# One kernel for tokenising, attention and a mixture of experts: the first tile of each expert at a fixed place, its loads and the list of tiles reordered, and the centring of the first layer norm moved behind the low half of the mix

## The chip, the cores and the metric

The kernel runs on one core of one Trainium2 chip. The metric is the device time of one execution in microseconds (us); lower is better. The time before is the median of three executions. Five engines work side by side: PE (TensorE, matmuls and transposes), DVE (VectorE), ACT (ScalarE), POOL (GpSimd) and SP (SyncE, which only issues transfers here). Sixteen DMA engines carry out all transfers.

## What is computed

`x` is (128, 750, 32). Everything is float32.

```python
h = patches(x, 16 rows, stride 8) @ W + b           # (128, 92, 128)
n = layernorm(h)                                    # over the last axis
s = einsum('bhie,bhje->bhij', n @ Wk, n @ Wq) / 64  # 8 heads
ax = einsum('bhtf,bhit->bhfi', n @ Wv, softmax(s))
h = h + reshape(ax) @ Wlt                           # (b, f, h*i) read as rows of 1024
t = layernorm(h)                                    # 11776 rows of 128
top2 of softmax(t @ Wr + br), renormalised          # 8 experts
h = h + sum over the two experts of weight * (relu(t @ W1[e] + b1[e]) @ W2[e] + b2[e])
```

## The kernel before

Operands that need float32 accuracy are split in a high half (type fp32r) and a low half, and a product is three matmuls: high by high, high by low, low by high (`three`, L331 to L335). So every intermediate is copied out of PSUM twice, by ACT as the high half and by DVE as the low half.

**First part (about 0 to 850 us), 32 groups of four sequences.** A group has eight steps, one for each sequence and half of the heads; `step(g, k, ...)` of each engine (PE L1387, ACT L801, DVE L1035, POOL L622, SP L448) writes its order out by hand, and different stages of different groups lie in one step. PE makes the scores (L1393), the mix with the probabilities (`mix`, L1405, lines L333 to L335), the transposes of the probabilities (L1418), the values (L1426), and, for the next group, the embedding (L1326), the transposes into token order (L1334) and back (L1340, `turn_xn`, in step 4). DVE in a step: sum of exponentials (L1040), row maximum (L1047), reciprocal (L1054), subtraction of the maximum (L1059), low half of the transposed probabilities (L1068, `probT_l`), low half of the mix (L1075, written into the memory of `w2s`, and so named in the profile). In step 2 it also takes the next group's layer norm moments (L985), its variance plus eps (`keep_var`, L991) and the centring of its tokens (`keep_xcent`, L997, `xcent`), both between L1059 and L1068:

```python
if k == 2 and exists(g + 1):
    keep_var(g + 1)
    keep_xcent(g + 1)
```

PE's mix waits for `probTl_kept` and for the low half of the mix before it (`mixl_kept`). POOL, in step 2, takes the variance to the power -0.5 (L599), multiplies the centred tokens by it (L606, `xtok`; waits for `xcent_kept`) and only then scales the probabilities (L592).

**Second part (about 850 to 1147 us), 23 chunks of 512 rows.** SP loads the chunk's rows and residual (`load_a`, L430, 2048 KB and 256 KB) one chunk ahead. It may issue chunk c+2 when h1 of chunk c is done. PE transposes and projects them, DVE adds the residual (`keep_h1`, L1104), and DVE and ACT do the second layer norm, the router, the top two and the rows' places (`posi`, L1183). `base` holds, for each expert, the row behind its last. Each expert has a room of ROOM = 12288 rows in `sorted_scratch`. POOL scatters the normalised rows of 520 bytes there, eight indirect transfers of 128 rows for each chunk (L709), with one pow between them (`root2`, L702). ACT may write `trow` of chunk c only when the scatters of chunk c-2 have landed (L872).

**The seam (about 1120 to 1156 us).** When the last chunk is counted, DVE copies `base` to `padi` (L1240); SP and ACT each write four pads of 512 blank rows behind the experts' last rows (`lay_pads`, L394 to L400, each with a register load). DVE and PE make the list of the 53 tiles of 512 rows (`whosei`: the expert, `wherei`: the first row; L1241 to L1255, PE L1522 to L1533): expert by expert, all tiles of one before those of the next. SP then (L505 to L521) waits for the list, loads the weights of the first tiles, waits for all pads, for the spare rows and for every scatter, and loads tiles 0 to 2. PE goes on at L1534 after the list, then waits for `posi`, `trow` and `res` of the last chunk.

**Third part (about 1156 to 1500 us), 53 tiles.** For each, SP copies one expert's weights inside SBUF (`w1t` L488, two buffers; `w2t` L495, three; 512 KB each) and loads the rows (`tin` L502, six buffers). In SP's order for tile n stand w2 of tile n+2, the rows of tile n+3, w1 of tile n+2 (L523). w1 of tile n+2 has to wait until the first layer of tile n is done. PE does transposes (L1543), first layer, second layer and transposes back (L1568); ACT and DVE the two halves of x and of the hidden layer; DVE weighs (L1278); POOL scatters the result (L734). In a **fourth part** (to the end) the two results of each row are read back and added to h.

Of the kernel before, what the change touches and what calls it, by code (L numbers as in the profile page):

```python
# [5 lines left out]
ALU = mybir.AluOpType  # L6
ACT = mybir.ActivationFunctionType
# [60 lines left out]
SETUP = 11  # L68
# [27 lines left out]
def build(nc, x, tok_w, tok_b, wq, wk, wv, wlt, wr, br, w1, b1, w2, b2, out):  # L96
# [8 lines left out]
    with ExitStack() as ctx, nc.allow_non_contiguous_dma("biases once"):  # L105
# [33 lines left out]

        arow0 = sb("arow0", [P, RT, H * D])  # L140
# [54 lines left out]
        wherei = sb("wherei", [1, TILES], I32)  # L195
        fillers = sb("fillers", [1, 2])
# [10 lines left out]
        square = sb("square", [P, RT, D], stack=second)  # L207
        lean = sb("lean", [P, RT], stack=second)
# [21 lines left out]
        held = sb("held", [P, NE], stack=second)  # L230
        starts = sb("starts", [P, 1], stack=second)
        holds = sb("holds", [P, NE], stack=second)
        jump = sb("jump", [P, NE], stack=second)
        tile_no = sb("tile_no", [TILES, 1], stack=second)
        past = sb("past", [TILES, NE], stack=second)
        jumps = sb("jumps", [TILES, NE], stack=second)
        ahead = sb("ahead", [TILES, 1], stack=second)
        entry = sb("entry", [TILES, 2], stack=second)
# [9 lines left out]
        hid_h = sb("hid_h", [P, FC, TT], F32R, stack=third)  # L248
        hid_l = sb("hid_l", [P, FC, TT], F32R, stack=third)
# [7 lines left out]
        yearly = raw.rearrange("p (s k r d) -> p s k r d", s=FIRST, k=2, r=RT)  # L257
# [6 lines left out]
        turn_ps, proj_ps, tok_ps, res_ps = (bank[0], bank[1], bank[4], bank[7]), bank[2], bank[3], bank[3]  # L264
        count_ps, logit_ps = bank[5], bank[6]
        lg_ps = logit_ps[:, 0:RT * (NE + 1)].rearrange("p (r e) -> p r e", r=RT)
        cum_ps, ntile_ps, row_ps = res_ps[:, 0:NE], res_ps[:, 64:64 + NE], bank[6][0:1, 0:3 * TILES]
# [37 lines left out]
        passed, counted, entries_kept, listed = (sem(n) for n in ("passed", "counted", "entries_kept", "listed"))  # L305
        padi_kept, holds_kept = sem("padi_kept"), sem("holds_kept")
# [107 lines left out]
        def _(sp):  # L414
# [60 lines left out]
            def chunk(c, i, q, more):  # L475
                if not isinstance(c, int) or c + 2 < NCH:
                    load_a(c + 2, i + 1, q)
                if isinstance(c, int) and c < NE:
                    sp.dma_start(w2raw[:, c, :, 1], w2[c].rearrange("(c p) d -> p c d", p=P)).then_inc(ws_2[c], 16)

            steps_second(sp, chunk)


            def load_w1(n, q):

                e = sp.value_load(whosei[0:1, bass.ds(n, 1)], min_val=0, max_val=NE - 1)
# [1131 lines left out]
```

## Time and profile before

| | us |
|---|---|
| median of three executions | 1559.43 (1559.01 to 1562.08) |
| the profiled execution, its own time | 1560.75 |
| its span, first to last instruction | 1558.7 |
| PE busy | 1402.7 (90%) |
| DVE busy | 1185.0 (76%) |
| ACT busy | 1018.3 (65%) |
| POOL busy | 802.7 (51%) |

The own time of the profiled execution is 2.05 us more than its span, which counts from the first to the last instruction. Busy shares are means over four parts with different limits, so the tables by stage and the chain of waits are of more use than they are. In a row of a timeline stand the start, the duration, the engine, the line, the operation and in brackets how long the engine had been idle and who ended it.

### The profile page before, as it was taken

To read this page: it belongs to the slowest core of one execution; us is meant where nothing else is said; L and a number is where in the kernel's file an instruction comes from. 1 tells how busy PE (TensorE), PEld (TensorE's weight loads), DVE (VectorE), ACT (ScalarE), POOL (GpSimd) and SP (SyncE) were. 2 spreads that over 40 slices of the span, in tenths; PEclk is the share of its full clock that TensorE was granted. 3 is DMA by queue.
4 is the path that set the end of the run, shared out by engine and by line. 5 is a ranking of instruction groups with operands and counts; after the bars stand their busy time and mean duration, and the time that the engine had idled before them with its cause. 6 is when DMAs were issued, how large, how long until landed. Compare 5 with 4: busy or idle time off the path is not lost.

```text
span 1558.7 us, 31914 instructions
## 1 busy us (share of the span) xinstructions
PE 1402.7 (90%) x7926; PEld 1136.2 (73%) x7926; DVE 1185.0 (76%) x3077; ACT 1018.3 (65%) x2282; POOL 802.7 (51%) x886
## 2 busy tenths in 40 slices
PE   4899999999999999999998999999849999999940
PEld 3677877787787788778776777777648888888830
DVE  1889898989889898988996788888736666666643
ACT  1587877877787787777785777777625555555510
POOL 1466343434434443443442577777735556666665
PEclk8999999999999999999998999999969999999975
DMA  3322222222222222222224788767356777666768
GB/s 81 129 74 89 74 96 83 88 82 78 87 73 90 89 88 81 79 87 73 87 92 173 254 273 278 258 228 249 145 203 243 249 251 248 244 245 243 250 207 309
DMA packets 114774, 247.45 MB, mean 159 GB/s; under 512 B 15376, under 2 KB 70816, under 8 KB 111776
## 3 DMA queue, kind: packets, MB, share of 16 engines
q1 hardware_dynamic: 92912, 206.43, 37.2%
q0 software_dynamic: 14368, 32.25, 6.4%
q10 hardware_dynamic: 7440, 8.15, 1.5%
q8 instruction: 22, 0.36, 0.1%
q14 instruction: 32, 0.26, 0.1%
HBM read 100.78 MB, written 90.43 MB: 123 GB/s over the span
## 4 chain that ended last, share of the span: by engine, by line
PE 66%; DVE 14%; issue 7%; DMA 7%; POOL 3%; ACT 2%; SPq 1%; DVEq 0%; POOLq 0%; ACTq 0%
PE bank L333 14%; PE bank L335 13%; PE bank L334 13%; PE bank L1393 7%; PE bank L1326 5%; PE bank L1418 4%; DVE w2s L1075 2%; PE bank L1458 2%; DMA hch<-h_scratch 2%; DVE probT_l L1068 2%; DMA sorted_scratch<-trow,posi 2%; DVE sixes L980 2%; PE bank L1543 2%; PE bank L1316 2%; PE bank L1568 2%
## 5 line engine op out<-in xcount | busy, mean ns | idle before, releaser
L592 POOL TENSOR_TENSOR prob<-expo,inv 92x368 f32<-92x368 f32 x256 | 204.6, 799 | 448.2 <-DVE inv L1054 448.2
L734 POOL DMA_INDIRECT y_scratch<-ytok,tin x212 | 204.9, 967 | 154.4 <-DVE ytok L1278 89.5
L1269 DVE SCALAR_TENSOR_TENSOR hid_l<-bank,hid_h 128x512 fp32r<-128x512 f32 x212 | 146.6, 692 | 130.2 <-ACT hid_h L921 130.2
L921 ACT ACTIVATE hid_h<-bank 128x512 fp32r<-128x512 f32 x212 | 126.8, 598 | 146.5 <-PE bank L335 146.5
L709 POOL DMA_INDIRECT sorted_scratch<-trow,posi x184 | 180.5, 981 | 68.2 <-issue 52.2
L1047 DVE TENSOR_REDUCE peak<-bank 92x4 f32<-92x368 f32 x256 | 136.1, 532 | 89.5 <-PE bank L1393 89.3
L1393 PE MATMUL bank<-z,xnT 128*92 128x368 f32 x512 | 200.5, 473 | 0.0
L781 ACT ACTIVATE z<-bank 128x368 f32<-128x368 f32 x256 | 122.2, 477 | 66.5 <-PE bank L335 59.4
L819 ACT ACTIVATE w2s<-bank 128x368 fp32r<-128x368 f32 x256 | 122.5, 479 | 62.1 <-PE bank L335 58.6
L826 ACT ACTIVATE expo<-cent 92x368 f32<-92x368 f32 x256 | 129.8, 507 | 26.0 <-DVE cent L1059 23.5
L1075 DVE TENSOR_TENSOR w2s<-bank,w2s 128x368 fp32r<-128x368 f32 x256 | 136.1, 531 | 6.3 <-ACT w2s L819 2.4
L333 PE MATMUL bank<-probT_h,xtok_h 92*128 92x368 f32 x256 | 114.2, 446 | 27.5 <-DVE w2s L1075 27.2
L1059 DVE TENSOR_TENSOR cent<-bank,peak 92x368 f32<-92x368 f32 x256 | 136.3, 532 | 1.0
L1068 DVE TENSOR_TENSOR probT_l<-bank,probT_h 92x368 fp32r<-92x368 f32 x256 | 134.6, 526 | 1.8 <-ACT probT_h L807 1.8
L1040 DVE TENSOR_REDUCE total<-expo 92x4 f32<-92x368 f32 x256 | 133.6, 522 | 0.4 <-ACT expo L826 0.3
L835 ACT ACTIVATE val<-bank 128x368 f32<-128x368 f32 x256 | 121.1, 473 | 18.0 <-PE bank L335 17.2
L1418 PE MATMUL bank<-ident,prob 92*92 92x92 f32 x1024 | 123.1, 242 | 0.2 <-POOL prob L592 0.2
L807 ACT ACTIVATE probT_h<-bank 92x368 fp32r<-92x368 f32 x256 | 119.7, 467 | 0.3
L1458 PE MATMUL bank<-ident,arow 128*128 128x128 f32 x736 | 113.2, 278 | 4.2 <-DMA hch<-h_scratch 4.1
L1418 PEld LDWEIGHTS bank<-ident,prob 92*92 92x92 f32 x1024 | 103.4, 124 | 18.5 <-issue 5.5
L1458 PEld LDWEIGHTS bank<-ident,arow 128*128 128x128 f32 x736 | 90.7, 145 | 33.4 <-DMA hch<-h_scratch 10.0
L1094 DVE TENSOR_TENSOR aT_l<-bank,aT_h 128x512 fp32r<-128x512 f32 x138 | 94.8, 691 | 25.0 <-ACT aT_h L858 23.5
(192 smaller groups left out, 3810.1 us busy)
## 6 DMA issues: line engine op xcount, KB each, us to landing
ax_scratch<-val SPq DMA_DIRECT2D x64, 736.0 KB, 3.5
arow<-ax_scratch SPq DMA_DIRECT2D x23, 2048.0 KB
w1t<-w1s SPq DMA_DIRECT2D x53, 512.0 KB, 3.5
w2t<-w2s SPq DMA_DIRECT2D x53, 512.0 KB, 3.0
tin<-sorted_scratch SPq DMA_DIRECT2D x53, 260.0 KB, 3.0
xin<-in_x_dram SPq DMA_DIRECT2D x32, 372.0 KB
arow<-y_scratch SPq DMA_DIRECT2D x24, 256.0 KB, 8.9
h_scratch<-hT SPq DMA_DIRECT2D x32, 184.0 KB, 7.1
```

The source lines that it names most:

```text
L333: mm(dst, wh, vh, start=start, stop=False)
L334: mm(dst, wh, vl, start=False, stop=False)
L335: return mm(dst, wl, vh, start=False, stop=stop)
L592: nc.gpsimd.tensor_tensor(prob[:, k % 2], expo[:, k % 2], inv[:, k % 2].unsqueeze(2).to_broadcast([S, HH, S]), ALU.mult).then_inc(prob_kep ...
L709: pool.indirect_dma_start(out=sorted_dram, out_offset=bass.IndirectOffsetOnAxis(ap=posi[:, q, choice, r:r + 1], axis=0), in_=trow[:, q, ch ...
L734: pool.indirect_dma_start(out=y_dram, out_offset=bass.IndirectOffsetOnAxis(ap=tin[:, b, r, D:D + 1].bitcast(I32), axis=0), in_=ytok[:, b % ...
L1068: V.tensor_tensor(probT_l[:, kt % 2], probT_ps[kt % 2][0:S, 0:GT].rearrange("j (h i) -> j h i", h=HH), probT_h[:, kt % 2].bitcast(F32), AL ...
L1075: V.tensor_tensor(mix_l[:, half * HH:(half + 1) * HH, b, :], mix_ps[:, 0:GT].rearrange("d (h i) -> d h i", h=HH), mix_h[:, half * HH:(half ...
L1269: V.scalar_tensor_tensor(hid_l[:, f], hid_ps[f][:], 0.0, hid_h[:, f].bitcast(F32), ALU.max, ALU.subtract).then_inc(hidl_kept, 1)
L1393: mm(score_ps[k % 2][0:S, 0:GT], xnT[:, q, b * S:(b + 1) * S], z[:, b, half * HH:(half + 1) * HH, :], start=True, stop=True).then_inc(scor ...
L1418: ins = nc.tensor.transpose(probT_ps[kt % 2][0:S, m * S:(m + 1) * S], prob[:, kt % 2, m], ident[0:S, 0:S])
L1458: ins = nc.tensor.transpose(turn_ps[j % TURNS][:, r * P:(r + 1) * P], arow[q][:, r, j * P:(j + 1) * P], ident[:])
```

## The change

In the first part, `keep_xcent(g + 1)` moves in DVE's step 2 from before L1068 to behind L1075. In the second, SP writes eight blocks of 512 blank rows at the experts' fixed first places during chunk 0, and POOL's first scatter waits for them; two iotas of POOL's setup go (SETUP 11 to 9), and POOL makes seven small constants in chunk 8 (`set_table`). DVE zeroes `mask_line` behind the first six `keep_aTl` and once the first part's stores are over. In chunk 21 DVE compares the least loaded expert, as counted through chunk 20, with 512 rows (`first_tiles_ready`, five small instructions). If it holds as many, SP waits for the scatters of chunks 0 to 20 only, otherwise for all.

Tiles 0 to 7 are now the first tiles of experts 0 to 7, at known rows and with known weights; the list is needed for the other 45 alone. SP loads the first weights without waiting for the list, ready or not, and the first three tiles behind the new wait. Then it waits for these to land, issues all eight pads itself, and waits for the pads in front of the rows of tile 3. For the list, for the spare rows and for all scatters it waits in front of the rows of tile 8. DVE makes the list alone, on one partition, behind its work for tiles 1, 2 and 3; PE's matmuls for it go. Some tiles get other places in memory, so that the pieces which now live at once don't overlap.

```diff
@@ SP, second part
+                if isinstance(c, int) and c == 0:
+                    sp.wait_ge(goal_kept, SETUP)
+                    for e in range(NE):
+                        sp.dma_start(sorted_dram[e * ROOM:e * ROOM + TT, :].rearrange("(p r) w -> p r w", p=P),
+                                     blank[:, e % 2]).then_inc(blanks_in, 16)
@@ SP, seam
             sp.wait_ge(proj_done, AC * NCH)
-            sp.wait_ge(h1_kept, NCH)
+            sp.wait_ge(h1_kept, NCH - 1)
             sp.wait_ge(low_kept, 2 * NE)
-            sp.wait_ge(ws_b2, 16)
-            lay_pads(sp, range(0, NE, 2))
-            sp.wait_ge(table, 1)
             for n in (0, 1):
                 load_w1(n, n)
                 load_w2(n, n)
             load_w2(2, 2)
-            sp.wait_ge(pads_in, 16 * NE)
-            sp.wait_ge(spares_in, 16 * SPARE)
+            sp.wait_ge(ready_kept, 5)
+            full = [16 * 2 * RT * ((NCH + 1 - half) // 2) for half in (0, 1)]
+            landed = [sp.value_load(ready[0:1, half:half + 1], ...) for half in (0, 1)]
             for half in (0, 1):
-                sp.wait_ge(scattered[half], 16 * 2 * RT * ((NCH + 1 - half) // 2))
+                sp.wait_ge(scattered[half], landed[half])
             load_tile(0, 0, 0)
             load_tile(1, 0, 1)
             load_tile(2, 0, 2)
+            for n in range(3):
+                sp.wait_ge(tile_in[n], 16)
+            lay_pads(sp, range(NE))
             def tile(n, i, q):
                 if not isinstance(n, int) or 3 <= n + 2 < TILES:
                     load_w2(n + 2, q + 2)
+                if isinstance(n, int) and n == 0:
+                    sp.wait_ge(pads_in, 16 * NE)
+                if isinstance(n, int) and n + 3 == NE:
+                    sp.wait_ge(table, 1)
+                    sp.wait_ge(spares_in, 16 * SPARE)
+                    for half in (0, 1):
+                        sp.wait_ge(scattered[half], full[half])
                 if not isinstance(n, int) or n + 3 < TILES:
                     load_tile(n + 3, i + (q + 3) // XRING, (q + 3) % XRING)
@@ POOL
+                if isinstance(c, int) and c == 0 and first == 0:
+                    pool_waits((blanks_in, 16 * NE))
                 if first == 0:
                     pool_waits((trow_kept, 2 * c + 2), (posi_kept, c + 1))
@@ ACT
-            lay_pads(act, range(1, NE, 2))
-            act.wait_ge(table, 1)
@@ DVE, first part
                 if k == 2 and exists(g + 1):
                     keep_var(g + 1)
-                    keep_xcent(g + 1)
...
                 if k == 1 and exists(g + 1):
                     keep_sixes(g + 1)
+                if k == 2 and exists(g + 1):
+                    keep_xcent(g + 1)
@@ DVE, chunk 21
+                nxt(V.tensor_tensor(held[:], base[0:1], ebase[0:1], ALU.subtract))
+                nxt(V.tensor_reduce(least[:, 0:1], held[:], AX_X, ALU.min))
+                nxt(V.tensor_scalar(least[:, 1:2], least[:, 0:1], float(TT), -16.0 * 2 * RT, ALU.is_ge, ALU.mult))
+                for half in (0, 1):
+                    V.tensor_scalar(ready[:, half:half + 1], least[:, 1:2], 16.0 * 2 * RT * ((NCH + 1 - half) // 2), None,
+                                    ALU.add).then_inc(ready_kept, 1)
@@ DVE, third part, behind the work of tile 2 (past and jumps are [1, 45, 8])
+                then(V.tensor_tensor(past[:], tile_no[:]..., cum[:]..., ALU.is_ge))
+                then(V.tensor_reduce(ahead[:], past[:], AX_X, ALU.add))
+                then(V.tensor_scalar(whosei[:, NE:TILES], ahead[:], float(NE - 1), None, ALU.min))
+                then(V.tensor_tensor(jumps[:], past[:], jump[:]..., ALU.mult))
+                then(V.tensor_reduce(ahead[:], jumps[:], AX_X, ALU.add))
+                then(V.scalar_tensor_tensor(ahead[:], tile_no[:], float(TT), ahead[:], ALU.mult, ALU.add))
+                V.tensor_scalar(wherei[:, NE:TILES], ahead[:], float(TT), None, ALU.add).then_inc(table, 1)
@@ PE, seam
-            pe.wait_ge(holds_kept, 1)
-            pe.wait_ge(trow_kept, 2 * NCH)
-            for k in range(NE):
-                mm(cum_ps[:, k:NE], ones[0:MOST, :], holds[0:MOST, 0:NE - k], start=k == 0, stop=k == NE - 1)
-            mm(ntile_ps, ones[0:MOST, :], holds[0:MOST, :], start=True, stop=True).then_inc(counted, 1)
...
-            pe.wait_ge(table, 1)
             pe.wait_ge(posi_kept, NCH)
             pe.wait_ge(trow_kept, 2 * NCH)
             pe.wait_ge(res_kept, NCH)
```

## Rows read from the trace of the kernel before

**Rows 1.** Page, section 4: the chain that ended last, by engine.

```profile
PE 66%; DVE 14%; issue 7%; DMA 7%; POOL 3%; ACT 2%; SPq 1%; DVEq 0%; POOLq 0%; ACTq 0%
```

**Rows 2.** Busy time by stretch: length, PE, PEld, DVE, ACT, POOL, PE clock, DMA share, GB/s.

```profile
120.00:835.00 715.00, 693.02 (x4125) 567.77 (x4124) 638.92 (x1698) 563.89 (x1296) 298.93 (x350) 1.00 0.24 86
...
900.00:1090.00 190.00, 180.03 (x1089) 141.34 (x1088) 160.77 (x567) 139.92 (x358) 144.69 (x150) 1.00 0.74 257
```

**Rows 3.** Who waited for whom: us in total, times, longest.

```profile
PE bank L333 <- DVE w2s L1075: 27.9, 40, 2.2
```

**Rows 4.** Timeline of DVE in one step 2 of the first part.

```profile
400.97 0.55 DVE L991 TENSOR_SCALAR varA<-moments 92x4 f32<-92x4 f32 x1
401.44 0.68 DVE L997 TENSOR_TENSOR xcent<-bank,moments 92x512 f32<-92x512 f32 x1
402.04 0.52 DVE L1068 TENSOR_TENSOR probT_l<-bank,probT_h 92x368 fp32r<-92x368 f32 x1
402.48 0.52 DVE L1075 TENSOR_TENSOR w2s<-bank,w2s 128x368 fp32r<-128x368 f32 x1
```

**Rows 5.** Timeline of PE in the same stretch.

```profile
401.70 0.78 PE L1393 MATMUL bank<-z,xnT 128*92 128x368 f32 x2
403.15 0.41 PE L333 MATMUL bank<-probT_h,xtok_h 92*128 92x368 f32 x1 [0.68 <-DVE w2s L1075]
...
406.13 0.48 PE L1340 MATMUL bank<-ident,xtok 92*128 92x92 f32 x4
```

**Rows 6.** Timeline of POOL in the same stretch.

```profile
402.82 1.04 POOL L606 TENSOR_TENSOR xtok<-xcent,rstdA 92x512 f32<-92x512 f32 x1
```

**Rows 7.** Timeline of POOL: the first and the last of 184 scatters of rows.

```profile
876.36 1.06 POOL L709 DMA_INDIRECT sorted_scratch<-trow,posi  x1 [7.88 <-DVE posi L1183]
...
1145.93 0.97 POOL L709 DMA_INDIRECT sorted_scratch<-trow,posi  x1 [0.30 <-issue]
```

**Rows 8.** Busy time by stretch, chunks 0 to 2 and the pads of before.

```profile
872.00:874.00 2.00, 1.90 (x18) 1.64 (x16) 1.97 (x5) 1.66 (x5) 0.00 (x0) 1.00 0.00 0
...
882.00:884.00 2.00, 2.00 (x11) 1.14 (x10) 1.83 (x9) 1.66 (x6) 1.39 (x3) 1.00 0.26 86
...
1137.00:1138.00 1.00, 1.00 (x6) 1.00 (x6) 0.00 (x0) 0.00 (x0) 0.97 (x1) 0.50 1.02 374
```

**Rows 9.** Timeline of SP: the load of chunk 3, and its four pads.

```profile
873.32 0.33 SPq L438 DMA_DIRECT2D arow<-ax_scratch  x1
...
1135.82 4.56 SPq L399 DMA_DIRECT2D sorted_scratch<-blank  x4
```

**Rows 10.** Timeline of PE: chunk 5 waits for its load.

```profile
908.86 0.66 PE L1458 MATMUL bank<-ident,arow 128*128 128x128 f32 x4 [2.03 <-DMA hch<-h_scratch]
```

**Rows 11.** Timeline of PE from the seam to tile 2.

```profile
1154.11 1.09 PE L1543 MATMUL bank<-ident,tin 128*128 128x128 f32 x4 [12.73 <-DMA tin<-sorted_scratch]
1156.69 0.79 PE L333 MATMUL bank<-x_h,w1t 128*128 128x512 f32 x1 [1.49 <-DVE x_l L1265]
...
1169.33 0.40 PE L333 MATMUL bank<-x_h,w1t 128*128 128x512 f32 x1
...
1173.11 0.48 PE L333 MATMUL bank<-hid_h,w2t 128*128 128x512 f32 x1
```

**Rows 12.** Timeline of DVE: the last places, and tile 2's first hidden block.

```profile
1134.50 0.18 DVE L1183 CAST posi<-posf 128x8 int32<-128x8 f32 x1
...
1170.86 0.69 DVE L1269 SCALAR_TENSOR_TENSOR hid_l<-bank,hid_h 128x512 fp32r<-128x512 f32 x1 [0.54 <-ACT hid_h L921]
```

**Rows 13.** Timeline of ACT: the last chunk's rows.

```profile
1129.44 1.93 ACT L875 ACTIVATE trow<-bank,shift,rstdB 128x254 f32<-128x254 f32 x4 [2.41 <-DVE shift L1130]
```

**Rows 14.** DMA issues: size, and median us from issue to landing.

```profile
w1t<-w1s SPq DMA_DIRECT2D x53, 512.0 KB, 3.5
...
sorted_scratch<-blank SPq DMA_DIRECT2D x4, 260.0 KB, 4.1
```

**Rows 15.** The centring in all groups: count, duration in ns, first and last start.

```profile
L997 DVE TENSOR_TENSOR xcent<-bank,moments x32: 674/676/680, 26.2 to 799.2; 92x512 f32<-92x512 f32 x32
```

More of the change, by code:

```diff
@@ L138, in build @@
         rank = sb("rank", [P, RT, NE])
+        hidden = ExitStack()
+        hid_h = sb("hid_h", [P, FC, TT], F32R, stack=hidden)
+        hid_l = sb("hid_l", [P, FC, TT], F32R, stack=hidden)
+        hidden.close()
         arow0 = sb("arow0", [P, RT, H * D])
@@ L229, in build @@
         ebase = sb("ebase", [P, NE], stack=second)
[L230 to L238, printed above, removed]
+        held = sb("held", [1, NE], stack=second)
+        starts = sb("starts", [1, MOST - 1], stack=second)
+        holds = sb("holds", [1, NE, MOST - 1], stack=second)
+        more_line = sb("more_line", [1, 2 * NE], stack=second)
+        cum = sb("cum", [1, NE], stack=second)
+        rooms = sb("rooms", [1, NE], stack=second)
+        least = sb("least", [1, 2], stack=second)
+        jump = sb("jump", [1, NE], stack=second)
+        tile_no = sb("tile_no", [1, REST], stack=second)
+        past = sb("past", [1, REST, NE], stack=second)
+        jumps = sb("jumps", [1, REST, NE], stack=second)
+        ahead = sb("ahead", [1, REST], stack=second)
         second.close()
@@ L722, in chunk @@
                     lay_spare(c)
+                if isinstance(c, int) and c == NE:
+                    set_table()
             steps_second(pool, chunk)
@@ L1240, in _ @@
             V.tensor_copy(padi[:], base[0:1, :]).then_inc(padi_kept, 1)
-            then(V.tensor_tensor(held[:], base[:], ebase[:], ALU.subtract))
-            V.tensor_scalar(holds[0:MOST], held[0:MOST], starts[0:MOST, 0:1], None, ALU.is_gt).then_inc(holds_kept, 1)
-            dve.wait_ge(counted, 1)
-            then(V.tensor_tensor(past[:], tile_no[:].to_broadcast([TILES, NE]), cum_ps[0:TILES], ALU.is_ge))
-            then(V.tensor_scalar(jump[:], ntile_ps, -float(TT), float(ROOM), ALU.mult, ALU.add))
@@ L1254, in _, with count_tiles @@
-            then(V.tensor_copy(whosei[:], row_ps[:, 0:TILES]))
-            V.tensor_copy(wherei[:], row_ps[:, TILES:2 * TILES]).then_inc(table, 1)
-            for half in (0, 1):
-                then(V.tensor_reduce(fillers[:, half:half + 1], row_ps[:, 2 * TILES + half:3 * TILES:2], AX_X, ALU.add))
-            for half in (0, 1):
-                V.tensor_scalar(real[:, half:half + 1], fillers[:, half:half + 1], -16.0 * TR,
-                                16.0 * TR * ((TILES + 1 - half) // 2), ALU.mult, ALU.add).then_inc(real_kept, 1)
+            def count_tiles():
+                dve.wait_ge(table_set, TABLE_SET)
+                then(V.tensor_tensor(held[:], base[0:1], ebase[0:1], ALU.subtract))
+                then(V.tensor_tensor(holds[:], held[:].unsqueeze(2).to_broadcast([1, NE, MOST - 1]),
+                                     starts[:].unsqueeze(1).to_broadcast([1, NE, MOST - 1]), ALU.is_gt))
+                then(V.tensor_reduce(more_line[:, NE:2 * NE], holds[:], AX_X, ALU.add))
+                line = more_line[:]
+                windows = bass.AP(tensor=line.tensor, offset=line.offset + 1, ap=[list(line.ap[0]), [1, NE], [1, NE]])
+                then(V.tensor_reduce(cum[:], windows, AX_X, ALU.add))
+                then(V.scalar_tensor_tensor(jump[:], more_line[:, NE:2 * NE], -float(TT), rooms[:], ALU.mult, ALU.add))
@@ L1263, in low_x, with count_fillers @@
+            def count_fillers():
+                for half in (0, 1):
+                    then(V.tensor_reduce(fillers[:, half:half + 1], past[:, half:REST:2, NE - 1], AX_X, ALU.add))
+                for half in (0, 1):
+                    V.tensor_scalar(real[:, half:half + 1], fillers[:, half:half + 1], -16.0 * TR,
+                                    16.0 * TR * ((TILES + 1 - half) // 2), ALU.mult, ALU.add).then_inc(real_kept, 1)
             def low_x(n, q):
```

102 lines of the change are left out of this document (66 added, 36 removed).

## The prediction

> **What bounds the kernel now.** I read the chain of waits first: PE has 66% of it and DVE 14% [rows 1], so a change counts where it shortens PE's waits, or DVE's work where DVE holds PE. The table by stretch then says where PE waits. In the first part it is busy 693.0 of 715 us [rows 2]: 22 us of idle over 29 groups, about 0.76 us each. The list of waits gives them a name: L333 behind DVE's L1075, 27.9 us in 40 waits [rows 3]. In the timeline it is one wait of 0.68 us in each group, in step 2, where DVE's work is longest [rows 4, 5]; from 154 to 801 us I counted 27 such waits of 0.58 to 0.70, and one of 2.21 at 130. In the second part all are close to full: PE 180.0 of 190 us, DMA share 0.74 [rows 2]. POOL issues 184 scatters in 270 us without a pause worth the name [rows 7], and PE at times waits for a load [rows 10]. Then comes the seam, where PE stands still until 1154.11 [rows 11]. From there to the end of the tiles it is full.
>
> **The centring.** Between the start of xcent and that of probT_l lie 0.60 us [rows 4]. Both operands of probT_l, and of the low half of the mix behind it, are there before (ACT made their high halves before 400.6), so both start 0.60 earlier, and PE's mix at 403.15 can start at 402.55 [rows 5]. The scores before it end near 402.47, so PE is still just held: the wait goes from 0.68 to about 0.08. DVE's next step starts when it did, as its sum of work is the same. Is the time kept? From 403.15 to 421.5 the chain is PE alone, and DVE waits for PE four times in a group, 2.6 us together; it can follow. Each group is worth 0.60: 28 x 0.60 = 16.8 us. The centring runs 32 times [rows 15]. One is ahead of the steps, and the other three lie in the first groups, where POOL is also splitting weights; I take 0.5 us for these three together. **-17.3.** Bounds: nothing (another wait stands right behind), and 31 x 0.68 = 21.
>
> What is late next: xcent ends at 403.0 in place of 402.1, so POOL's xtok goes from 402.82 to about 403.05 and ends at 404.1 [rows 6]. PE's turn_xn needs it at 406.13 - 0.60 = 405.5 [rows 5]: 1.4 us of cover.
>
> **Blanks in chunk 0.** SP issues eight more transfers of 260 KB, 2.13 MB, on its queue between the load of chunk 2 and that of chunk 3. While pads ran before, the engines moved 374 GB/s [rows 8]: 5.7 us. They were idle in 872 to 874 [rows 8], and the load of chunk 3 came at 873.3 [rows 9], so about 2 us are covered and 3.7 push that load. It was done near 883, when PE wanted it: the share of 0.26 in 882 to 884 [rows 8] is its end. So PE stands still 3.7 us. POOL's first scatter waits for the blanks as well, near 879 to 880 instead of 876.4, and since POOL then issues without pause [rows 7], it can't catch up either; root2 of chunk 1 stands behind the first two scatters. Both shifts are the same one. **+3.7**, between 0 (the load has cover that I don't see) and 8.3 (2.13 MB at the part's mean of 257 GB/s [rows 2]). PE's clock was at half at 1137 [rows 8], behind the short bursts and pauses that end the second part, and it came back some 3.4 us after the tiles began, which cost 1.7; a stand of 2.03 [rows 10] did not drop it. For one of 3.7 I take half the price, **+0.8**. The two iotas that go are not on the path: chunk 0's rows are only written at 870. set_table is seven instructions of about 0.15 us on a full POOL, in a chunk without a spare to lay: **+0.5** (0 to 1.1). mask_line is zeroed later but still before PE asks for it: nothing, the cover being chunk 0's own 11 us.
>
> **The seam.** SP can issue the five weight loads at 1120 instead of 1143. The scatters of chunk 20 had landed by 1129.4, as ACT's trow of chunk 22, which waits for them, then ran [rows 13]. So the three tiles are issued by about 1129.5 and here by 1133. PE is then held by its own wait for the last posi, 1134.7 [rows 12]; at its earliest it turns tile 0 at 1134.8 and not at 1154.11 [rows 11], 19.3 us sooner. Against that, 2.5 MB of weights now run beside the last scatters; trow of chunk 22, the exponential behind it on ACT, and through it the last posi may come later. Unloaded, a scatter takes some 2 to 4 us to land, beside the loads of the second part 6.4 to 7.3 in the chain; that would be up to 3 us. I take 1136.0: **-18.1** (-19.3 to -16). PE's 18 small matmuls for the list go and cost nothing.
>
> The Trainium skill (DMA: Bandwidth & Descriptors, Queues, rings and completion order) says that each DMA engine goes round between the queues packet by packet. By that rule the scatters wait for at most a packet and the start would be near 1135, one us better; the loaded landings above speak for more, and the sum keeps 1136.
>
> **The pads** are the new wait. Four took 4.56 us on SP [rows 9], 1.39 apart; ACT no longer takes half. The first goes out 1.1 after posi, 1137.1; the eighth 9.7 later, landed 4.1 after that [rows 14]: 1150.9. Behind this wait on SP stand the rows of tile 3 and w1 of tile 2: issued 1151.4, landed 3.5 later [rows 14], 1154.9. PE wants w1 of tile 2 12.64 us after its first matmul (1156.69 to 1169.33 [rows 11]), and that is at 1136.0 + 2.6: 1151.2. **+3.7** (0 to 6), and **+0.8** for PE's clock as above. Rows of tile 3, w2 of tile 3 and w1 of tile 3 follow in time.
>
> **DVE's list.** Chunk 21: five small instructions, some 1 us, **+0.3**, as DVE waits 1.9 us for POOL soon after. In the tiles: about 1.3 us behind tile 1, covered by the stand. Behind tile 2 four operations of 360 columns (0.52 like those of 368 [rows 4]) and three small ones (0.2 [rows 12]), 2.7 us. DVE has 0.5 free there, and tile 2's low half, done at 1171.55, is used at 1173.11 [rows 11, 12]: 1.5 of cover. 2.7 - 0.5 - 1.5 = **+0.7**. Behind tile 3 less than the cover. Above: varA took 0.55 for four columns [rows 4], while POOL scaled probabilities, so an instruction of this kind can be held by POOL. The skill's page SBUF — State Buffer (Two separate sides) states this as an exclusive lock of the port that DVE and GpSimd share. By that rule all fourteen could take up to 0.4 more, 3 us in the sum after cover; posi, beside POOL's issues, took 0.18 [rows 12], so I add nothing.
>
> **Sum:** -17.3 + 3.7 + 0.8 + 0.5 - 18.1 + 3.7 + 0.8 + 0.3 + 0.7 = -24.9. Against the profiled execution's own 1560.75 (span 1558.7 and 2.05 around it) that is 1535.9. This execution stands 1.3 above the median of 1559.43, so I say 1534.5.
>
> **Rivals.** A measurement of this kernel tells about 0.2%, 3.1 us, from no change.
> *The centring buys nothing* (0.12): another wait stands behind the first, such as the low half of the mix one step on, where PE had no more than 0.2 us in hand. For it: several DVE and ACT results arrive in step 4 just as PE takes them. Against: these follow PE, which is itself earlier. 1534.5 + 17.3 = 1552; with half the gain 1543.
> *The start is not brought forward* (0.05): one expert has under 512 rows after chunk 20, so SP waits for every scatter; the change then doesn't do what it says. 21 chunks give 21504 rows, 2688 for an expert; it would need one at a fifth of that. 1534.5 + 18.1 = 1553.
> *The blanks and pads cost their upper bounds* (0.13): the load of chunk 3 comes 8.3 late and w1 of tile 2 by 6. 1534.5 + 4.6 + 2.3 = 1541.4.
> *They cost nothing* (0.10), both being hidden: 1534.5 - 3.7 - 0.8 - 3.7 - 0.8 = 1525.5.
> *Slower* (0.02): xtok, behind the later centring, is late for turn_xn in step 4. If it ends 1.4 us later than I have it, it begins to eat the gain; at 2.0 the gain is gone (406.13 - 404.1); to end above 1562.5 it must also give back the other 7.6 us and 3.1 more, 10.7 / 31 = 0.35 for each group, so end 2.4 later. If it ends 2.5 later, the time is 1552 + 31 x 0.5 = 1567.5. For it: DVE and POOL have slowed each other here (varA). Against: xtok takes 1.04 [rows 6], and only the pow is queued before it.
>
> **Numbers.** The forecast has 0.58 with its own range of 1530 to 1540. 1526 to 1547 takes in it, the case of the upper bounds, half a centring and all but the edge of the cheap case; left out are the two cases at 1552 and 1553 and the slower one. Faster 0.96, within 0.2% 0.02, slower 0.02.
>
> **What would show it.** Right: groups of 24.3 us instead of 24.9, L333's wait under 0.2; one stand of some 4 us near chunk 2; the first turn of tile 0 near 1136 - 17.3 + 5.0 = 1124, and one PE wait for w1 before tile 2's first layer. Wrong: a group still of 24.9; POOL's last scatter not about 12 us earlier; a first turn 15 us later than that.

## The result, and the profile after

| | before | after |
|---|---|---|
| median of the runs compared | 1560.64 us (4 runs) | 1532.89 us (4 runs) |
| lowest to highest | 1559.01 to 1562.08 | 1531.93 to 1536.34 |
| ratio | 1 | 0.9826 [0.9807, 0.9846] |
| profiled execution: own time, span | 1560.75, 1558.7 | 1533.04, 1530.9 |

Forecast: 1534.5 us, between 1526 and 1547, faster. Measured: 1532.89, so 1.6 us under the forecast and inside the range; faster by 1.7%.

The page of the changed kernel: busy time of PE, the chain by engine, and the mix's first matmul in the table of groups (busy us, mean ns, then the idle time before it with its releaser).

```profile
PE 1401.2 (92%) x7902; PEld 1132.8 (74%) x7902; DVE 1180.4 (77%) x3082; ACT 1017.2 (66%) x2282; POOL 801.9 (52%) x891
...
PE 73%; DMA 9%; DVE 6%; issue 5%; POOL 4%; ACT 2%; SPq 1%; POOLq 0%; DVEq 0%; ACTq 0%
...
L342 PE MATMUL bank<-probT_h,xtok_h 92*128 92x368 f32 x256 | 114.1, 446 | 9.9 <-DVE w2s L1126 7.1
```

DVE's share of the chain fell from 14% to 6% and PE's rose from 66% to 73% [rows 1]. The helper's three matmuls are now L342, L343 and L344, and the low half of the mix is L1126. The wait that stood at 27.9 us in 40 waits [rows 3] is 7.8 in 12 in the same view, 7.1 of it in the group shown, and what is left lies in the first groups (until 128 us) and in the last (from 799 us), not in the steady ones.

Where the 27.8 us of span went, from milestones that both traces have (the step h of chunk 0, its last run in chunk 22, the last posi, the first turn of tile 0, the last turn of results, the end):

| stretch | before | after | difference | forecast |
|---|---|---|---|---|
| start to h of chunk 0 | 860.88 | 843.19 | -17.69 | -17.3 |
| to h of chunk 22 | 260.69 | 266.27 | +5.58 | +5.3 |
| to the last posi | 12.93 | 12.95 | +0.02 | +1.2 |
| to the first turn of tile 0 | 19.61 | 0.23 | -19.38 | -19.3 |
| to the last turn of results | 342.87 | 345.46 | +2.59 | +5.2 |
| to the end of the span | 61.7 | 62.8 | +1.08 | 0 |
| sum | | | -27.8 | -24.9 |

The timeline of DVE, first in a step 2 of the first part, then at the seam.

```profile
393.11 0.55 DVE L1043 TENSOR_SCALAR varA<-moments 92x4 f32<-92x4 f32 x1
393.58 0.53 DVE L1119 TENSOR_TENSOR probT_l<-bank,probT_h 92x368 fp32r<-92x368 f32 x1
394.03 0.52 DVE L1126 TENSOR_TENSOR w2s<-bank,w2s 128x368 fp32r<-128x368 f32 x1
394.48 0.67 DVE L1049 TENSOR_TENSOR xcent<-bank,moments 92x512 f32<-92x512 f32 x1
...
1120.38 0.37 DVE L1213 TENSOR_REDUCE upto<-mask_line 128x32 fp32r<-128x128 f32 x1
...
1122.41 0.17 DVE L1236 CAST posi<-posf 128x8 int32<-128x8 f32 x1
```

The centring stands behind the low half of the mix. The distance from varA to the start of that half is 0.92 us, where it was 1.51 [rows 4].

The timeline of PE: the same step 2, chunk 1, the seam, and the two places in the tiles where it waits (the bracket is idle time before the instruction, with its releaser).

```profile
393.84 0.78 PE L1481 MATMUL bank<-z,xnT 128*92 128x368 f32 x2
394.70 0.40 PE L342 MATMUL bank<-probT_h,xtok_h 92*128 92x368 f32 x1
...
397.69 0.48 PE L1428 MATMUL bank<-ident,xtok 92*128 92x92 f32 x4
...
866.79 0.66 PE L1546 MATMUL bank<-ident,arow 128*128 128x128 f32 x4 [1.05 <-DMA hch<-h_scratch]
869.38 0.40 PE L1579 MATMUL bank<-mask_line,before_r 128*128 128x40 f32 x1 [1.94 <-DVE upto L1213]
...
1120.81 0.40 PE L1579 MATMUL bank<-mask_line,before_r 128*128 128x40 f32 x1 [8.59 <-DVE upto L1213]
1121.04 0.37 PE L1581 MATMUL bank<-upto,ones_r 128*128 128x32 f32 x1
1122.64 1.12 PE L1618 MATMUL bank<-ident,tin 128*128 128x128 f32 x4 [1.22 <-DVE posi L1236]
1125.22 0.80 PE L342 MATMUL bank<-x_h,w1t 128*128 128x512 f32 x1 [1.47 <-DVE x_l L1347]
...
1139.35 0.48 PE L342 MATMUL bank<-x_h,w1t 128*128 128x512 f32 x1 [1.29 <-issue]
...
1150.28 0.47 PE L342 MATMUL bank<-hid_h,w2t 128*128 128x512 f32 x1 [0.42 <-DVE hid_l L1351]
```

At 394.70 the 0.68 us bracket of [rows 5] is gone. At 1122.64 the 12.73 us wait for the rows of tile 0 [rows 11] is 1.22, and its releaser is the last posi: PE now starts as early as its own wait lets it.

The timeline of POOL: xtok behind the later centring, the first scatter, the rstdB (root2) of chunk 1, the last scatter.

```profile
393.82 1.00 POOL L635 TENSOR_TENSOR rstdA<-varA,power 92x4 f32<-92x4 f32 x1 [0.18 <-DVE varA L1043]
395.23 1.04 POOL L642 TENSOR_TENSOR xtok<-xcent,rstdA 92x512 f32<-92x512 f32 x1 [0.40 <-DVE xcent L1049]
...
862.24 1.06 POOL L756 DMA_INDIRECT sorted_scratch<-trow,posi  x1 [11.46 <-issue]
...
864.62 1.06 POOL L747 TENSOR_TENSOR rstdB<-varB,power 128x4 f32<-128x4 f32 x1
...
1133.83 0.97 POOL L756 DMA_INDIRECT sorted_scratch<-trow,posi  x1 [0.30 <-issue]
```

xtok ends at 396.27 and PE takes it at 397.69: 1.42 us of cover.

The timeline of SP: the eight blanks, the load of chunk 3, the weights and rows of the first tiles, the pads, and w1 of tile 2.

```profile
845.69 5.88 SPq L493 DMA_DIRECT2D sorted_scratch<-blank  x8
855.66 0.34 SPq L447 DMA_DIRECT2D arow<-ax_scratch  x1
...
1108.42 0.60 SPq L512 DMA_DIRECT2D w1t<-w1s  x1
...
1118.79 1.30 SPq L530 DMA_DIRECT2D tin<-sorted_scratch  x3
1124.27 8.48 SPq L408 DMA_DIRECT2D sorted_scratch<-blank  x8
1135.16 0.34 SPq L530 DMA_DIRECT2D tin<-sorted_scratch  x1
1135.56 0.50 SPq L512 DMA_DIRECT2D w1t<-w1s  x1
```

The three tiles are issued at 1118.79, 15 us before POOL issues its last scatter; before, they came behind all of them.

Busy time by stretch (length, PE, PEld, DVE, ACT, POOL, granted PE clock, DMA share, GB/s): the first part, chunks 1 and 2, the start of the tiles, and the stand at tile 2.

```profile
120.00:818.00 698.00, 692.26 (x4120) 566.71 (x4118) 634.23 (x1697) 562.45 (x1293) 296.59 (x349) 1.00 0.25 88
...
866.00:868.00 2.00, 0.66 (x4) 0.42 (x4) 1.71 (x9) 1.83 (x4) 1.70 (x2) 1.00 0.37 109
868.00:870.00 2.00, 0.62 (x3) 0.62 (x4) 1.87 (x7) 0.97 (x3) 1.39 (x3) 0.82 0.10 33
870.00:872.00 2.00, 2.00 (x11) 2.00 (x11) 1.86 (x9) 1.00 (x3) 1.69 (x2) 0.50 0.62 157
...
876.00:878.00 2.00, 2.00 (x13) 1.65 (x12) 1.07 (x3) 1.64 (x6) 0.44 (x1) 0.97 0.92 312
...
1138.00:1140.00 2.00, 0.71 (x4) 0.58 (x4) 1.86 (x7) 0.00 (x0) 0.32 (x1) 1.00 1.01 381
```

In the first part PE is idle for 5.7 us of 698, where it was 22 of 715 [rows 2].

### The profile page after: what moved, and what is told of

It is laid out like the page before. It is cut to its first block, busy times and chain, and to the rows that moved or that the text cites. A ratio compares the mean times of both kernels' runs of the same rounds, so it can differ in the third digit from the quotient of the medians.

```text
span 1530.9 us, 31767 instructions
## 1 busy us (share of the span) xinstructions
PE 1401.2 (92%) x7902; PEld 1132.8 (74%) x7902; DVE 1180.4 (77%) x3082; ACT 1017.2 (66%) x2282; POOL 801.9 (52%) x891
## 3 DMA queue, kind: packets, MB, share of 16 engines
q1 hardware_dynamic: 94640, 209.63, 38.6%
## 4 chain that ended last, share of the span: by engine, by line
PE 73%; DMA 9%; DVE 6%; issue 5%; POOL 4%; ACT 2%; SPq 1%; POOLq 0%; DVEq 0%; ACTq 0%
PE bank L342 16%; PE bank L344 15%; PE bank L343 15%; PE bank L1481 9%; PE bank L1414 5%; PE bank L1506 5%; DMA hch<-h_scratch 3%; DMA sorted_scratch<-trow,posi 2%; POOL sorted_scratch L756 2%; PE bank L1404 2%; PE bank L1618 2%; PE bank L1643 1%; DMA out_dram<-outs 1%; PE bank L1546 1%; PE bank L1422 1%
## 5 line engine op out<-in xcount | busy, mean ns | idle before, releaser
L1126 DVE TENSOR_TENSOR w2s<-bank,w2s 128x368 fp32r<-128x368 f32 x256 | 136.2, 532 | 5.4 <-ACT w2s L868 2.5
L342 PE MATMUL bank<-probT_h,xtok_h 92*128 92x368 f32 x256 | 114.1, 446 | 9.9 <-DVE w2s L1126 7.1
```

What stands on the lines that cost most here:

```text
L342: mm(dst, wh, vh, start=start, stop=False)
```

## The experiments

Two theories stood against each other for each of the three edits: that the time goes where the prediction's step puts it, and that another edit, or another wait of the same edit, has it. Nine kernels were run, three of them twice. Each diff is against the changed kernel unless it says otherwise. The first four ran where the kernel before took 1563.47 us (median of 7 runs). The other eight ran where it took 1710.28 (1 run) and 1702.21 (median of 11). There the transfers moved 199 to 208 GB/s from 900 to 1100 us, against 253 in the changed kernel's trace; the last section says what is known of this. Of those eight only stretches are read. Up to h of chunk 2 they keep the times of the other runs within 1.4 us, but for one first part; from there on single chunks take 12 to 20 us in all of them, with an edit or without. (Interval 1 below is from h of chunk 0 to h of chunk 1, and so on. In the kernel before they are 11.27, 11.39, 12.02, 12.00, in the changed one 11.26, 14.79, 14.18, 11.54.)

**Centring alone**, in the kernel before:

```diff
                     keep_var(g + 1)
-                    keep_xcent(g + 1)
...
                 if k == 1 and exists(g + 1):
                     keep_sixes(g + 1)
+                if k == 2 and exists(g + 1):
+                    keep_xcent(g + 1)
```

> The kernel before with the centring alone moved behind the low half of the mix. Theory A (each group's step 2 held PE by DVE, and the centring was 0.60 us of it): groups of 24.3 us, 17 to 18 us less than before, ratio near 0.989. Rival B (the gain of the first part comes from elsewhere, such as the new places of tiles in memory): groups stay at 24.9, time as before.

1544.80 us, ratio 0.9877 [0.9853, 0.9900]: 18.7 us. h of chunk 0 ran at 843.0 instead of 860.9, groups took 24.28 us, and the chunks had their old intervals: 11.27, 11.40, 11.97. The seam was the old one:

```profile
1137.87 1.09 PE L1544 MATMUL bank<-ident,tin 128*128 128x128 f32 x4 [13.27 <-DMA tin<-sorted_scratch]
```

**The rest alone**: the changed kernel with the centring back ahead of probT_l.

```diff
                     keep_var(g + 1)
+                    keep_xcent(g + 1)
...
-                if k == 2 and exists(g + 1):
-                    keep_xcent(g + 1)
```

> The changed kernel with the centring back at its old place. Theory A: the parts add up, so 17 to 18 us more than the changed kernel, near 1550.5, ratio to before near 0.993; everything behind the first part as in the changed kernel. Rival B: no more than 3 us more.

1553.48 us, ratio 0.9929 [0.9906, 0.9952]: 10.0 us under before. Groups took 24.85 us, the first intervals 11.25, 14.80 and 14.20, and the first turn came 0.22 us behind the last posi. The two halves give 18.7 and 10.0 us, 28.7 together; the whole gives 27.75. They add up, so neither hides part of the other.

**How far must the centring go?** Once behind probT_l but ahead of the low half of the mix, once a whole step later:

```diff
+                if k == 2 and exists(g + 1):
+                    keep_xcent(g + 1)
                 gm, km = back(g, k, LAG_M)
...
-                if k == 2 and exists(g + 1):
-                    keep_xcent(g + 1)
```

```diff
-                if k == 2 and exists(g + 1):
+                if k == 3 and exists(g + 1):
                     keep_xcent(g + 1)
```

> The changed kernel with the centring between the low half of the probabilities and the low half of the mix. Theory A as I now state it: PE's mix waits for both low halves and the low half of the mix is the last of them, so nothing is gained: groups of 24.9, near 1550. Rival C: PE can start its mix on the low half of the probabilities and needs the other later, so half or all of the gain stays: 1533 to 1542.

> The changed kernel with the centring one step later still (step 3, behind the low half of the mix). This prices the rival of the prediction that ends slower. By the prediction's cover of 1.4 us between the end of xtok and PE's transpose of it, a centring some 3 us later overruns it by 1.6 and also holds POOL's scaling of the probabilities behind it: 1 to 2 us for each group, 30 to 60 in all, 1563 to 1593, above the kernel before. Rival: PE has other work to do in the meantime and the time stays within 5 us of the changed kernel.

The half-way place: 1556.02 us, groups of 24.87, as if the centring had never moved. The timeline of PE has the old wait back, whole:

```profile
154.89 0.78 PE L1481 MATMUL bank<-z,xnT 128*92 128x368 f32 x2
156.34 0.41 PE L342 MATMUL bank<-probT_h,xtok_h 92*128 92x368 f32 x1 [0.67 <-DVE w2s L1128]
```

The gain hangs on one order only: what PE's mix waits for last is the low half of the mix, and the centring must not stand ahead of it. (Both places of this pair are one execution each.) The late place: 1569.47 us, slower than before by 6. Groups took 25.35, which is 1.07 above the changed kernel's. The timelines of DVE, PE and POOL in one group:

```profile
383.69 0.52 DVE L1126 TENSOR_TENSOR w2s<-bank,w2s 128x368 fp32r<-128x368 f32 x1
...
386.49 0.67 DVE L1049 TENSOR_TENSOR xcent<-bank,moments 92x512 f32<-92x512 f32 x1
```

```profile
388.33 0.54 PE L1428 MATMUL bank<-ident,xtok 92*128 92x92 f32 x4 [0.93 <-POOL xtok L642]
```

```profile
387.24 1.03 POOL L642 TENSOR_TENSOR xtok<-xcent,rstdA 92x512 f32<-92x512 f32 x1 [2.84 <-DVE xcent L1049]
```

A step later is 2.35 us later: xcent starts 2.80 us behind the start of step 2's low half of the mix, where the changed kernel has 0.45 (394.03 to 394.48). xtok ends 4.58 behind that start instead of 2.24. Of these 2.34 us the cover takes 1.42, and the 0.92 that is left is PE's wait of 0.93. The other 0.14 of the group's 1.07 was not taken apart. This is the prediction's slower rival brought about: it is real, and the change stops 1.4 us short of it.

**All scatters waited for again** at the seam, everything else as changed:

```diff
-            landed = [sp.value_load(ready[0:1, half:half + 1], ...) for half in (0, 1)]
...
-                sp.wait_ge(scattered[half], landed[half])
+                sp.wait_ge(scattered[half], full[half])
```

> The changed kernel, but SP waits for all 184 scatters before the first tiles. Theory A (the start of the tiles was set by the last scatters, and the wait for 16 fewer of them is what brings it forward): the last scatter is issued near 1133.8 and lands 4 us later, tiles are there 3 us after that, first turn near 1141 instead of 1122.6, 18 to 19 us more than the changed kernel, near 1551. Rival D (the list, made by DVE with PE's help and followed by the weight loads, was the last wait, and taking it off the path is the gain): 5 us more at most, near 1538.

> SP waits for all 184 scatters before the first tiles, again. Theory A: first turn of a tile about 7.5 us behind the start of the last scatter, not 11 ahead of it, so 18 to 19 us more than the changed kernel, near 1551. Rival D (the list was the last wait): 5 us more at most, near 1538.

From the last posi to the first turn: 16.75 and 16.74 us, where the changed kernel has 0.23 and the other runs with the shorter wait 0.22 to 0.25, but for one with 0.63 (the blanks in the first four groups). The timeline of SP, then of PE:

```profile
1202.62 1.30 SPq L530 DMA_DIRECT2D tin<-sorted_scratch  x3
```

```profile
1205.60 1.08 PE L1617 MATMUL bank<-ident,tin 128*128 128x128 f32 x4 [17.74 <-DMA tin<-sorted_scratch]
```

POOL's last scatter was issued at 1200.27; the rows follow it by 2.35 and PE's turn by 5.33. So 16.5 of the 19.4 us are the wait for the last scatters, where 18 to 19 were expected. The other 2.9 (19.61 - 16.75) are what the kernel before had in that stretch beside it, its pads, list and weight loads together; these were not taken apart.

**No blanks in chunk 0** (rows that no token fills are then left as they are), twice:

```diff
-                if isinstance(c, int) and c == 0:
-
-                    sp.wait_ge(goal_kept, SETUP)
-                    for e in range(NE):
-                        sp.dma_start(sorted_dram[e * ROOM:e * ROOM + TT, :]...)
...
-                    pool_waits((blanks_in, 16 * NE))
```

> The changed kernel without the eight blank blocks in chunk 0 and without POOL's wait for them (it leaves out only the filling of first tiles that would not be full). Theory A: the second part loses the 5.6 us that it took longer: two chunks of 11.4 and 12.0 instead of 14.8 and 14.2, near 1527.5. Rival: part of the 5.6 is from set_table and the instructions of chunk 21, so less than 4 us come back.

> The edit of the kernel without blank blocks again (it leaves out only the filling of first tiles that would not be full), on a chip with faster transfers. Theory A: two intervals of 11.4 and 12.0 at the start of the second part instead of 14.8 and 14.2, near 1527.5. Rival: less than 4 us come back.

Interval 2 was 11.30 in both, and the first scatter came 15.44 and 15.43 us behind h of chunk 0: before's 11.39 and 15.48, where the changed kernel has 14.79 and 19.05. (Interval 3 was 14.97 and 17.74 and can't be read here, as ACT and DVE stand still in it for 2 to 3 us at a time, with the releaser that the last section speaks of; that it too is long because of this half of the change shows in the first two experiments, 11.97 without it and 14.20 with it.) set_table was still in this kernel, so my +0.5 for it is not in intervals 1 and 2. The timeline of POOL:

```profile
858.10 1.07 POOL L748 DMA_INDIRECT sorted_scratch<-trow,posi  x1 [7.85 <-DVE posi L1228]
859.47 0.99 POOL L748 DMA_INDIRECT sorted_scratch<-trow,posi  x1 [0.30 <-issue]
860.48 1.05 POOL L741 TENSOR_TENSOR rstdB<-varB,power 128x4 f32<-128x4 f32 x1
```

posi ran at 857.01 here and rstdB of chunk 1 at 860.48, 3.47 behind; in the changed kernel at 857.62 and 864.62, 7.00 behind.

**The same eight transfers to rows that nobody reads**, with no wait on POOL, twice. This keeps the pushed load and takes POOL's late start away:

```diff
-                        sp.dma_start(sorted_dram[e * ROOM:e * ROOM + TT, :]...
+                        sp.dma_start(aside_dram[e * TT:e * TT + TT, :]...
...
-                    pool_waits((blanks_in, 16 * NE))
```

> The changed kernel with the same eight transfers of 260 KB at the same place, written to memory that nobody reads, so POOL need not wait for them. Theory A (two paths of the same length: the load of chunk 3 is pushed, and POOL starts late): the load is still pushed, so at most 1 us comes back, near 1532. Rival E (POOL's late start alone costs, as it never pauses again): 4 to 5 us come back, near 1528.

> The blank blocks written aside with no wait of POOL, again. As the first two intervals of the earlier look were 11.7 and 13.0, I now hold with rival E for the larger part: the pushed load costs 1 to 1.5 us and POOL's late start the other 4, so near 1529. Theory A of the prediction, two paths of the same length, would leave 1532.

Interval 2 was 11.68 and 11.37, and the first scatter 15.75 and 15.45 behind h. With the blanks in place, on the same two occasions, interval 2 was 15.21 and 15.72. So what lengthens interval 2 is POOL's late start, and not the pushed load. The other runs agree: in each of the fourteen traces interval 2 is the distance from h of chunk 0 to the first scatter less 4.1 to 4.3 us, from 11.30 for 15.43 without blanks to 15.96 for 20.20 with the half-way centring, whose blanks took 7.30 us on SP. PE did wait for the load, a little later:

```profile
866.14 0.66 PE L1545 MATMUL bank<-ident,arow 128*128 128x128 f32 x4 [1.50 <-DMA hch<-h_scratch]
```

That is inside interval 3, which was 12.95 and 13.25 against before's 12.02. The first of the two is free of the long occasion's waits until its end, so the load by itself costs some 0.9 us there; the second has one of 1.79 in it. And the busy time by stretch shows PE's clock whole behind this single wait (column as above, 1.00):

```profile
864.00:866.00 2.00, 0.64 (x2) 0.00 (x0) 1.80 (x6) 0.82 (x3) 1.70 (x2) 1.00 0.89 291
866.00:868.00 2.00, 1.86 (x18) 1.86 (x18) 0.54 (x1) 1.17 (x3) 1.39 (x3) 1.00 0.71 185
868.00:870.00 2.00, 2.00 (x16) 1.82 (x17) 1.79 (x11) 1.08 (x3) 1.28 (x2) 1.00 0.99 303
```

**The blanks in the first four groups**, two experts in each, from one row per partition that POOL makes at the start. The eight transfers of chunk 0 go, and POOL's wait stays:

```diff
+                if isinstance(g, int) and g < WARM and k in (1, 5):
+                    e = 2 * g + k // 4
+                    sp.wait_ge(blank_set, 2)
+                    sp.dma_start(sorted_dram[e * ROOM:e * ROOM + TT, :]...,
+                                 first_blank[:].unsqueeze(1).to_broadcast([P, TR, ROWW])).then_inc(blanks_in, 16)
```

> The changed kernel with the eight blank blocks written in the first four groups, from a block of its own of one blank row on each partition. The DMA engines are a third busy there. Theory A: 5 to 6 us less than the changed kernel, near 1527.5, the first part unchanged. Rival: the 2.13 MB delay the loads of x or the stores of h in the first groups, and the gain is given back there.

Intervals 1 and 2 were 11.25 and 11.37, the first scatter 15.45 behind h: the cost in interval 2 is gone. h of chunk 0 came only at 849.4, and the irregular groups (24.7 to 25.4) lay between the 7th and the 21st and once near the 30th, where no blank is written; the second run without any blanks has two such groups as well (25.04 and 24.63). The next kernel has the same edit and had h of chunk 0 at 844.0. So the first part doesn't have to pay, but this is one profile each.

**All three together**: blanks early, w1 of tile 2 ahead of the wait for the pads, and the list spread over tiles 2 and 3 and its end over tile 4.

```diff
                 if isinstance(n, int) and n == 0:
+                    load_w1(2, 2)
                     sp.wait_ge(pads_in, 16 * NE)
...
-                if not isinstance(n, int) or n + 2 < TILES:
+                if not isinstance(n, int) or 0 < n < TILES - 2:
                     load_w1(n + 2, q + 2)
...
                 if isinstance(n, int) and n == 2:
-                    list_tiles()
+                    list_experts()
                 if isinstance(n, int) and n == 3:
+                    list_rows()
+                if isinstance(n, int) and n == 4:
                     count_fillers()
```

> The changed kernel with three edits: the blank blocks are written in the first four groups; w1 of tile 2 is issued in front of the wait for the pads; DVE's list is spread over tiles 2 and 3. Theory A: 5.6 us less in the second part (its first intervals near 11.4 and 12.0), 1.5 less at tile 2 (no wait for w1, distance from tile 1 near 6.4) and 0.7 less at tile 3: near 1525 where the changed kernel has 1533, ratio to before near 0.977. Rival: the blank blocks only move their cost to the first groups, whose sum grows by as much, and the time is within 2 us of the changed kernel.

1672.13 us (median of 6) against 1702.21 (of 11), ratio 0.9810 [0.9757, 0.9863]. The interval holds both the changed kernel's 0.9826 and the expected 0.977, so it decides nothing. Intervals 1 and 2 were 11.25 and 11.37, and the first turn came 0.23 behind posi; the start of the tiles can't be read: the eight pads took 16.32 us on SP, and PE waited 1.83 and 2.61 us behind work of ACT and DVE that itself came late (ACT's x_h with the releaser that the last section speaks of). Whether this version beats the changed kernel on an occasion near 1560 us stays open. By the changed kernel's own stretches it has at most the 5.6 us of the second part and some 2 in the tiles to take back.

## Why the prediction was right, step by step

**The centring: right, -17.69 for -17.3**, and for the reason given. The wait of 0.68 in each group is gone, groups went from 24.87 to 24.28, and 28 times 0.59 is 16.5; the rest is from the first groups. The cover of xtok was put at 1.4 and measured at 1.42. The first experiment shows that the edit alone brings it, the half-way place that it is the order against the low half of the mix, and the late place that the slower rival was sized about rightly: with xtok 2.34 late against a cover of 1.42 it puts 0.92 on each group, PE waited 0.93, and the group lost 1.07.

**Blanks: the sum was right, its terms were not.** Forecast 3.7 + 0.8 + 0.5 and 0.3 for chunk 21, 5.3; measured 5.58. That these agree is in part luck. The step that failed is the one that makes the load of chunk 3 late by 3.7 and has PE stand 3.7 for it, with POOL's late start as the same shift. PE waited only 1.05 us for the load (866.79). What held it was the other path: the first scatter 3.57 late against h of chunk 0, rstdB of chunk 1 behind two such scatters just as late, `upto` (DVE's sum over the chunk's marks, the last step before PE's part of the places) behind that, and PE at 869.38. Interval 2 is 3.40 longer, which is POOL's delay. The wait for the load lies inside it, since without it PE would have stood at upto that much sooner; the experiment with the load alone leaves interval 2 at its old length. So the delay was well sized and put down to the wrong queue.

The clock was undersized: I gave half of 1.7. The granted clock was 0.82 in 868 to 870 and then 0.50, the lower of the two levels (1.2 GHz), until 876. Interval 3 is 2.16 longer, with PE busy in it without a gap from 869.8 on, and intervals 4 and 5 give 0.73 back. Busy time by stretch, interval 3 before and then after:

```profile
883.54:895.56 12.02, 11.62 (x71) 8.85 (x69) 10.31 (x37) 8.84 (x23) 9.67 (x11) 1.00 0.83 284
```

```profile
869.24:883.42 14.18, 14.04 (x67) 11.81 (x68) 10.38 (x38) 8.98 (x23) 9.91 (x12) 0.76 0.71 241
```

PE was busy 2.4 us longer on the same work (a trace can lack some matmul records, hence 71 and 67) at a mean clock of 0.76; its eight small router matmuls, for one, took 1.72 us where they had taken 0.96. The same drop is in the run without the centring, behind waits of 1.67 and 1.29. That it is the clock that lengthens interval 3 is read from these rows and from the load-alone run, whose clock stayed at 1.00; no run took the clock's share by itself. The +0.5 of set_table did not show. Another 0.76 came in small pieces over the later chunks, and chunk 21's own +0.3 can't be told from them: its interval was 13.14 for 12.97, but 13.14 too with the centring alone.

**The seam: mechanism right, 1.3 too little.** Forecast -18.1 with bounds of -19.3 and -16, measured -19.4, the better bound itself. The term that was mis-sized is the 1.2 us for last scatters that land late beside the weight loads. The weights were issued from 1108.42 on, and ACT's trow of chunk 22, which waits for the scatters of chunk 20, ran at 1118.85, about 5.4 us after the last of them had gone out; before it ran 5.1 ahead of the last posi, here 3.6 ahead. That is the lateness I feared, 1.5 us, but the exponential behind it came only 0.2 late to its reader, and the last posi not at all: 12.95 us behind the last h, where it was 12.93. DVE's own chain of small instructions set posi, not ACT. The Trainium skill's rule (DMA: Bandwidth & Descriptors, Queues, rings and completion order), that a DMA engine goes round its queues packet by packet, would have given "near 1135", which is the better number; but these rows don't prove the rule, as trow was late and only its effect was covered.

**Pads: +1.5 for +3.7, and no +0.8.** The wait before tile 2 was there (1139.35), as forecast: SP held w1 of tile 2 until the pads had landed. The terms, counted from PE's first matmul of the tiles (1125.22): the first pad went out 0.95 ahead of it for 1.5, the eight took 8.48 us for 9.7 (1.2 apart, not 1.39), landed some 2.4 later for 4.1, and w1 was usable 3.8 after its issue for 3.5. That is 14.13 against 12.64 wanted, 1.5. The interval from turn to turn is 7.92 where before had 6.39. And a wait of 1.3 did not touch the clock: 1.00 in 1138 to 1140.

**DVE's list: right.** The interval of the tile behind it is 7.05 for 6.37, 0.68 where 0.7 was forecast, with the wait where it was put (1150.28, for hid_l). The Trainium skill (SBUF — State Buffer, SBUF: two separate sides) has an exclusive lock of the port pair that DVE and GpSimd share. Laid on all the small instructions, as the prediction did when it weighed it, that would have made some 3 us more; no such delay is in this trace, where the list's four wide operations took 0.51 to 0.52 us each and its small ones 0.18, 0.20 and 0.44.

**Not foreseen:** 1.08 us more from the last turn of results to the end, and some 0.4 elsewhere in the tiles. Nothing was tried on them. They are open.

The terms for the pads (2.2), the clock at tile 2 (0.8), the seam (1.3) and the centring (0.4) were all too careful, 4.7 us together; the second part (0.3), the rest of the tiles (0.4) and the tail (1.1) took back 1.8. That is the 2.9 us between -24.9 and -27.8. The time itself is only 1.6 under the forecast, because the forecast also took off 1.3 for a profiled execution above its median, and the changed kernel's stands just 0.15 above its own. None of the rivals occurred: the time lies in the forecast's own range.

## What to carry to other kernels

Before moving an instruction behind another, look for the one operand that the bounding engine waits for last; here both places tried ahead of the low half of the mix gave nothing and the first place behind it gave everything, with 1.4 us to go until the next reader was late. When rows at fixed places let a consumer start early, look at who waits for what the shorter wait needs: the eight blanks cost little through the loads that they pushed, and 3.4 us through the wait that they put ahead of POOL's first scatter, with rstdB, DVE and PE behind it. And where a full PE is made to stand, price its clock too.

## What the runs showed of the hardware that I had not expected

- **The clock.** PE's granted clock fell to half after waits of 1.05 and 1.94 us with about 0.7 us of work between them, and again in the run without the centring after 1.67 and 1.29. It stayed whole behind single waits of 2.03 (in the kernel before, [rows 10]), 1.50 and 1.29, and fell behind a single one of 4.05 (second run without blanks). Where it fell after two short waits it came back only some 6 us later, though PE had been busy all the while.
- **The long occasions did not have slower transfers.** The same kernel before took 1560.64, 1563.47, 1702.21 and 1710.28 us. In the changed kernels of the long occasions the first posi still ran at 856.2 to 858.5 (one at 863.8), against 857.62; the loss lies behind it, where the transfers had moved 253 GB/s and now moved 199 to 208. But the packets of the main queue took 38.6% of 1530.9 us in the changed kernel, 591 us, and 35.5% of 1672.1 with all scatters waited for, 594 us: by this measure they were as fast as ever, with more idle time between them. What the eight long traces have, and none of the other six has, is 44 to 53 waits of ACT and DVE, 78 to 92 us together, whose releaser the profile gives only as "remote". The timeline of ACT in the second run without blanks has the first of them:

```profile
871.61 0.60 ACT L925 ACTIVATE h1tok<-bank 128x512 f32<-128x512 f32 x1 [3.11 <-remote]
```

What stands behind that name is open. The eight pads took 16.3 us on SP beside the last scatters there, and 8.00 where all scatters had landed first. So stretches can be compared across such runs as long as no such wait lies in them, and sums can't.
